# Attention keys in chunks of 512, six key products ahead, and another order on TensorE

## The chip, the cores and the metric

One core of one Trainium2 chip runs the whole program in one launch. The metric is the device time of an execution in microseconds (us), lower is better. Engines are called TensorE (PE in the profile, PEld its weight loads), VectorE (DVE), ScalarE (ACT), GpSimd (POOL) and SyncE (SP).

## What is computed

The reference is one block of three parts over x (2 sequences of 64 rows of 256) and a context (2 sequences of 1024 rows of 256). The change touches the first part alone, a cross attention with 16 heads of 64 and one learned null key and value:

```python
q = x_normed @ Wq;  k, v = split(ctx @ Wkv)
q, k = tanh(q), tanh(concat(null_key, k))
attn = softmax(q @ k.T * 64 ** -0.5)
x = x + (attn @ concat(null_value, v)) @ Wout + bout
```

Then follow a gated linear attention and a mixture of 8 experts (2 per row), each with its own normalisation and residual. Their code stays as it is.

## The kernel before

The attention never forms the values. For each head it sums the context rows themselves, weighted with the exponentials of the scores (mixT), and multiplies by the value weights once at the end (`values`, L1166).

The work is cut into **steps**. A unit is a batch b, a chunk c of CK = 256 keys and a group g of 8 heads; there are 16 units. Each unit has KT = 2 steps, one for each 128 keys, so there are 32 steps. Each step has three jobs on TensorE:

- `project_keys(kp)` (L1104), a **key product**: two head pairs by the chunk's 256 keys into one PSUM bank (two banks, in turn). Operands are split into a high and a low part, and three products (high-high, high-low, low-high; `split_product`, L1097) over two halves of the 256 inputs make 12 matmuls of 256 columns.
- `scores(s)` (L1123): 16 small f16 matmuls, 128 keys by the 8 heads' queries, into one of two score banks.
- `weighted_sum(s)` (L1140): 6 matmuls of 512 columns, split likewise, the context rows (ctx_h, ctx_l) by the exponentials (ex_h, ex_l), accumulated in four banks.

ScalarE follows with `keys_tanh` (L611: a tanh in PSUM and two copies to f16, the keys' high half) and `exponentials` (L654: the same exponential written twice). VectorE follows with `low_keys` (L793: the keys' low half, two instructions), `low_exponentials` (L849: the low part of the exponentials at L765, and their sum at L822), the casts of arriving context chunks to their high part (`high_ctx`, L778, for the weighted sums; `high_ctxT`, L771, transposed, for the key products) and `evacuate` (L804: finished sums out of PSUM). GpSimd makes the chunks' low parts (`low_ctx`, L518; `low_ctxT`, L514), in the order in which VectorE casts them. Chunks lie in two buffers each, in turn. SyncE issues their loads, between those of later weights.

Every engine's order is written out by hand; each runs its list in program order, and semaphores tie them. A key product waits until its bank's last keys have their low half (`k_ready`), a score step for its bank (`el_ready`, `esum_ready`), a weighted sum for the exponentials' low part and for its context chunk:

```python
                pe.wait_ge(el_ready, s + 1)
                pe.wait_ge(ctx_ready, n + 1)
```

Before the first score, AHEAD = 3 key products are done. The first four steps run singly: scores, a key product, a weighted sum (L1221). From then on TensorE's order in a pair of steps is scores, key products (three ahead), weighted sums of the pair before (L1231 to L1241). The pairs are numbered here from 0; pair u holds steps 2u and 2u+1, and is unit u. VectorE's list has the casts in `convert_context` (L857), behind each unit's low halves.

At the start x is normalised (VectorE, L762), transposed by TensorE, copied out of PSUM (`xnT`, L833) and multiplied by the query weights (L1200). TensorE fills the time before that with matmuls of no use (`warm`, L1086).

## Time and profile before

| | us |
|---|---|
| median of 3 runs | 204.99 |
| lowest and highest | 203.99, 205.06 |
| the profiled execution | 204.92 |
| its span in the profile | 203.0 |
| attention, first query product to the values | 8.0 to 124.2 |

The profile holds one execution. Its page gives busy times by engine and by line; its timelines give the start and duration of each instruction, with the idle time ahead of it and what ended that in brackets. Durations of matmuls overlap, since they are pipelined, so the distance between two starts tells what one costs in a stream.

### The profile page before, as it was taken

The numbers are of one execution on the slowest core, as the hardware profiler recorded it, in microseconds if no ns is written. First come the engines' busy times: TensorE is split into PE (matmuls) and PEld (weight loads), VectorE is DVE, ScalarE is ACT, GpSimd is POOL, SyncE is SP. The second block draws the span as 40 slices with busy tenths as digits, with TensorE's granted clock in tenths as the row PEclk, the third lists the DMA queues.
The fourth block names the chain that finished last, engine by engine and source line by source line (L and its number), as shares of the span: only waits on it lengthen the run. The fifth ranks groups of instructions, "written<-read, shape, count | busy, mean of one in ns | idle before, by whom it ended". The sixth has DMA issues, their size and how long they took to land.

```text
span 203.0 us, 4247 instructions
## 1 busy us (share of the span) xinstructions
PE 192.7 (95%) x1667; PEld 147.0 (72%) x1669; DVE 142.5 (70%) x259; ACT 116.2 (57%) x217; POOL 47.4 (23%) x48
## 2 busy tenths in 40 slices
PE   7999889999999999999999999999986999999991
PEld 2698779988998889988998767866753454544680
DVE  2679899989888899999878699435777825404313
ACT  2389999777977798778877672026430133222200
POOL 5636024220222062202202950021321300000001
PEclk9999999999999999999999999999999699999998
DMA  6945984934691110010000799999999400000000
GB/s 207 390 110 128 281 187 118 365 108 124 185 343 35 52 52 3 0 55 0 5 0 2 242 386 264 386 375 377 381 377 378 150 0 3 0 0 0 5 0 26
DMA packets 20836, 30.95 MB, mean 152 GB/s; under 512 B 1841, under 2 KB 15570, under 8 KB 20818
## 3 DMA queue, kind: packets, MB, share of 16 engines
q1 hardware_dynamic: 20098, 29.12, 44.1%
q10 hardware_dynamic: 720, 1.57, 2.1%
q8 instruction: 13, 0.21, 0.4%
q14 instruction: 5, 0.04, 0.1%
HBM read 29.51 MB, written 0.13 MB: 146 GB/s over the span
## 4 chain that ended last, share of the span: by engine, by line
PE 59%; issue 21%; DVE 11%; ACT 4%; POOL 2%; DMA 2%; POOLq 0%; DVEq 0%; ACTq 0%
PE ps L1101 39%; PE ps L1135 6%; PE ps L1200 2%; DVE keys L799 2%; PE ps L1175 2%; PE ps L1191 2%; PE ps L1089 2%; DVE att L949 2%; DMA x<-in_x 2%; DVE ex_sum L822 1%; ACT keys L621 1%; DVE ex_l L765 1%; PE ps L1163 1%; DVE lo L974 1%; PE ps L1312 1%
## 5 line engine op out<-in xcount | busy, mean ns | idle before, releaser
L799 DVE SCALAR_TENSOR_TENSOR keys<-ps,keys 64x512 f16<-64x512 f32 x64 | 44.1, 688 | 2.9 <-ACT keys L621 0.9
L621 ACT ACTIVATE keys<-ps 64x512 f16<-64x512 f32 x64 | 37.9, 593 | 1.8
L1101 PE MATMUL ps<-ctxT_h,w_k_h 128*128 128x256 f32 x128 | 37.9, 296 | 0.0
L1101 PE MATMUL ps<-ctxT_h,w_k_l 128*128 128x256 f32 x128 | 36.2, 282 | 0.0
L1101 PE MATMUL ps<-ctxT_l,w_k_h 128*128 128x256 f32 x128 | 36.1, 282 | 0.0
L765 DVE TENSOR_TENSOR ex_l<-ps,ex_h 128x512 fp32r<-128x512 f32 x32 | 22.0, 688 | 9.7 <-ACT ps L661 9.6
L660 ACT ACTIVATE ex_h<-ps 128x512 fp32r<-128x512 f32 x32 | 19.1, 597 | 13.9 <-PE ps L1135 13.7
L1101 PE MATMUL ps<-ex_h,ctx_h 128*128 128x512 f32 x64 | 25.3, 396 | 0.0
L1101 PE MATMUL ps<-ex_l,ctx_h 128*128 128x512 f32 x64 | 25.1, 392 | 0.0
L1101 PE MATMUL ps<-ex_h,ctx_l 128*128 128x512 f32 x64 | 24.9, 389 | 0.0
L1101 PEld LDWEIGHTS ps<-ctxT_h,w_k_h 128*128 128x128 f32 x128 | 24.4, 191 | 0.2
L1101 PEld LDWEIGHTS ps<-ctxT_l,w_k_h 128*128 128x128 f32 x128 | 24.5, 191 | 0.1
L1101 PEld LDWEIGHTS ps<-ctxT_h,w_k_l 128*128 128x128 f32 x128 | 24.4, 191 | 0.0
L822 DVE TENSOR_TENSOR ex_sum<-ex_sum,ps 128x512 f32<-128x512 f32 x32 | 21.7, 678 | 0.0
L1135 PEld LDWEIGHTS ps<-q_two,keys 128*128 128x128 f16 x512 | 16.0, 98 | 6.4 <-DVE keys L799 4.9
L505 POOL TENSOR_TENSOR ctx_l<-stage_n,ctx_h 128x512 fp32r<-128x512 f32 x8 | 10.3, 1294 | 42.4 <-DVE ctx_h L783 42.4
L1135 PE MATMUL ps<-q_two,keys 128*128 128x64 f16 x512 | 18.2, 193 | 1.8 <-DVE keys L799 1.1
L617 ACT ACTIVATE ps<-ps 128x512 f32<-128x512 f32 x32 | 18.4, 576 | 1.5 <-PE ps L1101 1.2
L661 ACT ACTIVATE ps<-ps 128x512 f32<-128x512 f32 x32 | 19.1, 598 | 0.0
L505 POOL TENSOR_TENSOR ctxT_l<-stage_t,ctxT_h 128x512 fp32r<-128x512 f32 x7 | 9.2, 1312 | 29.7 <-DVE ctxT_h L776 29.7
L1089 PE MATMUL ps<-warmer 128*128 128x512 bf16 x41 | 14.6, 500 | 1.5 <-POOL warmer L499 1.3
L1101 PEld LDWEIGHTS ps<-ex_h,ctx_h 128*128 128x128 f32 x64 | 12.1, 189 | 3.7 <-issue 1.6
(189 smaller groups left out, 272.9 us busy)
## 6 DMA issues: line engine op xcount, KB each, us to landing
w<-in_fc1T SPq DMA_DIRECT2D x8, 1024.0 KB, 12.4
w<-in_fc SPq DMA_DIRECT2D x8, 1024.0 KB, 12.3
stage_n<-in_ctx SPq DMA_DIRECT2D x8, 256.0 KB, 2.9
stage_t<-in_ctxT SPq DMA_DIRECT2D x7, 256.0 KB, 4.4
q_two<-q_split SPq DMA_DIRECT2D x8, 128.0 KB, 2.3
w_v<-in_Wv SPq DMA_DIRECT2D x1, 1024.0 KB, 5.4
w_out<-in_Wout SPq DMA_DIRECT2D x1, 1024.0 KB, 8.1
const<-in_const SPq DMA_DIRECT2D x1, 968.0 KB, 6.6
```

The lines of the kernel that those rows point to most:

```text
L505: return nc.gpsimd.tensor_tensor(dst, full, high.bitcast(F32), ALU.subtract)
L617: nc.scalar.activation(full, full, ACT.Tanh).then_inc(k_tanh, 1)
L621: nc.scalar.activation(keys[rows, u % 2, PK * i:PK * (i + 1), r], full[rows].rearrange("p (j n) -> p j n", j=PK), ACT.Copy, scale=UNIT).th ...
L660: nc.scalar.activation(ex_h[:, r], full, ACT.Exp, scale=SCORE_SCALE)
L661: nc.scalar.activation(full, full, ACT.Exp, scale=SCORE_SCALE).then_inc(e_ready, 1)
L765: return V.tensor_tensor(dst, full, high.bitcast(F32), ALU.subtract)
L799: V.scalar_tensor_tensor(out=keys[other, u % 2, PK * i:PK * (i + 1), r], in0=ps[mine, K_BANK + kp % 2].rearrange("p (j n) -> p j n", j=PK) ...
L822: V.tensor_tensor(total, total, ps[:, S_BANK + s % 2].rearrange("p (h q) -> p h q", q=S), ALU.add).then_inc(esum_ready, 1)
L949: V.copy_predicated(dst, mask, src).then_inc(att_ready, 1)
L1089: MM(ps[:, bank], warmer[:, 0:P], warmer[:], start=True, stop=True)
L1101: last = MM(dst, lhs[i], rhs[j], start=start and m == 0, stop=stop and m == len(parts) - 1)
L1135: last = MM(ps[:, S_BANK + s % 2, (2 * j + r) * S:(2 * j + r + 1) * S], keys[:, u % 2, j, r, t * P:(t + 1) * P], q_two[:, g, r, part, j, b ...
```

## The change

Key products and the transposed context now go by chunks of CK = 512 keys, so that there are 8 units of KT = 4 steps and still 32 steps. A key product is one head pair by 512 keys: 6 matmuls of 512 columns. The context rows of the weighted sums keep chunks of CN = 256 keys, eight of them, numbered over both batches; a weighted sum of step s reads chunk n = 2 (b NC + c) + t // 2. The key weights stay in four pieces, each now used by two key products.

AHEAD is 6, and all 16 pairs v run alike: TensorE does scores of steps 2v and 2v+1, weighted sums of steps 2v-2 and 2v-1, then key products 2v+6 and 2v+7. VectorE's casts and evacuations follow from three small tables, by the pair behind which they stand. The identity matrix is now loaded first from ScalarE's queue, no longer from SyncE's, and the copy of xnT is ScalarE's. The buffers for transposed chunks double in size.

```diff
@@ -40,14 +40,18 @@
...
-CK = 256
+CK = 512
+CN = 256
...
+NN = NK // CN
+KN = CN // P
...
+PIECES = 4
@@ -143,16 +147,16 @@
...
-        w_k_stage = alloc(attn_a, "w_k_stage", [P, G * KT, DC, PK * P])
+        w_k_stage = alloc(attn_a, "w_k_stage", [P, PIECES, DC, INNER // PIECES])
...
-        stage_n = alloc(attn_a, "stage_n", [P, 2, KT, D])
+        stage_n = alloc(attn_a, "stage_n", [P, 2, KN, D])
...
@@ -367,8 +371,8 @@
...
-        AHEAD = KT + 1
-        SINGLES = G * KT
+        AHEAD = KT + 2
+        PAIRS = STEPS // 2
@@ -400,7 +404,7 @@
...
         def ctx_source(n):
-            return a["ctx"][n * CK:(n + 1) * CK].rearrange("(t p) d -> p t d", p=P)
+            return a["ctx"][n * CN:(n + 1) * CN].rearrange("(t p) d -> p t d", p=P)
@@ -432,7 +436,6 @@
...
             sp.dma_start(x0[:], a["x"]).then_inc(ld_x, 16)
-            sp.dma_start(const[:, 0:C_ONES], a["eye"]).then_inc(ld_eye, 16)
@@ -451,12 +454,9 @@
...
-            load_ctxT(4)
             load_ctx(3)
...
-            load_ctxT(5)
-            load_ctx(4)
@@ -470,15 +470,13 @@
...
-            for n in range(5, B * NC):
-                if n + 1 < B * NC:
-                    load_ctxT(n + 1)
+            for n in range(4, B * NN):
                 load_ctx(n)
...
-                    sp.wait_ge(ctx_ready, B * NC)
+                    sp.wait_ge(ctx_ready, B * NN)
@@ -529,29 +527,31 @@
...
-                    for i in range(G * KT):
+                    for i in range(PIECES):
...
+                    low_ctx(0)
...
-                    low_ctx(0)
-                    for i in range(1, B * NC):
-                        if i + 1 < B * NC:
-                            low_ctxT(i + 1)
+                    low_ctx(1)
+                    pool.wait_ge(zero_ready, 1)
+                    pool.wait_ge(null_ready, 2)
+                    pool.wait_ge(ctx_ready, 2)
+                    for r in range(2):
+                        sums, mine = null_rows(1, r)
+                        nc.gpsimd.tensor_copy(sums, mine).then_inc(null_sums, 1)
+                    pool.wait_ge(null_sums, 2)
+                    low_ctxT(2)
+                    low_ctx(2)
+                    low_ctx(3)
+                    low_ctxT(3)
+                    low_ctx(4)
+                    pool.wait_ge(esum_ready, STEPS // B)
+                    pool.wait_ge(ctx_ready, 5)
+                    for r in range(2):
+                        sums, mine = null_rows(0, r)
+                        nc.gpsimd.tensor_tensor(sums, sums, mine, ALU.add).then_inc(null_sums, 1)
+                    pool.wait_ge(null_sums, 4)
+                    for i in range(5, B * NN):
...
-                        if i == 1:
-                            pool.wait_ge(zero_ready, 1)
-                            pool.wait_ge(null_ready, 2)
-                            pool.wait_ge(ctx_ready, i + 1)
-                            for r in range(2):
-                                sums, mine = null_rows(1, r)
-                                nc.gpsimd.tensor_copy(sums, mine).then_inc(null_sums, 1)
-                            pool.wait_ge(null_sums, 2)
-                        if i == NC:
-                            pool.wait_ge(esum_ready, STEPS // B)
-                            pool.wait_ge(ctx_ready, i + 1)
-                            for r in range(2):
-                                sums, mine = null_rows(0, r)
-                                nc.gpsimd.tensor_tensor(sums, sums, mine, ALU.add).then_inc(null_sums, 1)
-                            pool.wait_ge(null_sums, 4)
@@ -635,6 +635,7 @@
...
+            act.dma_start(const[:, 0:C_ONES], a["eye"]).then_inc(ld_eye, 16)
             act.dma_start(stage_t[:, 0], ctxT_source(0)).then_inc(ld_ctxT[0], 16)
@@ -642,6 +643,8 @@
...
             split_wk(0)
+            act.wait_ge(xnT_psum, 1)
+            copy(xnT[:], ps[:, 0, 0:DC * P].rearrange("p (c t) -> p c t", c=DC), xnT_ready)
             split_wk(1)
@@ -649,7 +652,8 @@
...
-            keys_tanh(2)
+            for kp in range(2, AHEAD):
+                keys_tanh(kp)
@@ -660,15 +664,12 @@
...
-            for s in range(SINGLES):
-                exponentials(s)
-                if s < G:
-                    null_exp(s)
-                keys_tanh(s + AHEAD)
-            for u in range(SINGLES // KT, NU):
-                for s in range(KT * u, KT * (u + 1)):
-                    exponentials(s)
-                for kp in range(KT * u + AHEAD, min(KT * (u + 1) + AHEAD, STEPS)):
+            for v in range(PAIRS):
+                exponentials(2 * v)
+                if v < G:
+                    null_exp(v)
+                exponentials(2 * v + 1)
+                for kp in range(2 * v + AHEAD, min(2 * v + AHEAD + 2, STEPS)):
                     keys_tanh(kp)
@@ -779,7 +780,7 @@
...
-                    dve.wait_ge(mix_done, G * KT * (n - 1))
+                    dve.wait_ge(mix_done, KT * (2 * ((n - 2) // 2) + 1) + KN * (n % 2) + KN)
@@ -829,8 +830,6 @@
...
-            dve.wait_ge(xnT_psum, 1)
-            V.tensor_copy(xnT[:], ps[:, 0, 0:DC * P].rearrange("p (c t) -> p c t", c=DC)).then_inc(xnT_ready, 1)
@@ -842,9 +841,11 @@
...
-            high_ctxT(1)
             high_ctx(0)
             low_keys(2)
+            high_ctxT(1)
+            for kp in range(3, AHEAD):
+                low_keys(kp)
@@ -854,27 +855,20 @@
...
-            def convert_context(u):
-                b, c, g = units[u]
-                n = b * NC + c
-                if g == 0 and n + 2 < B * NC:
-                    high_ctxT(n + 2)
-                if g == G - 1 and n + 1 < B * NC:
-                    high_ctx(n + 1)
-
-            for s in range(SINGLES):
-                low_exponentials(s)
-                low_keys(s + AHEAD)
-                if s % KT == KT - 1:
-                    convert_context(s // KT)
-            for u in range(SINGLES // KT, NU):
-                for s in range(KT * u, KT * (u + 1)):
+            next_ctx = {0: 1, 4: 2, 5: 3, 8: 4, 9: 5, 12: 6, 13: 7}
+            next_ctxT = {3: 2, 7: 3}
+            left = {7: 2, 9: 3}
+            for v in range(PAIRS):
+                for s in range(2 * v, 2 * v + 2):
                     low_exponentials(s)
-                for kp in range(KT * u + AHEAD, min(KT * (u + 1) + AHEAD, STEPS)):
+                for kp in range(2 * v + AHEAD, min(2 * v + AHEAD + 2, STEPS)):
                     low_keys(kp)
-                convert_context(u)
-                if units[u - 2][1] == NC - 1:
-                    evacuate(u - 2)
+                if v in next_ctxT:
+                    high_ctxT(next_ctxT[v])
+                if v in next_ctx:
+                    high_ctx(next_ctx[v])
+                if v in left:
+                    evacuate(left[v])
@@ -1109,14 +1103,15 @@
...
-                pe.wait_ge(wk_ready[KT * g + i], 1)
+                piece, half = 2 * g + i // 2, i % 2
+                pe.wait_ge(wk_ready[piece], 1)
...
-                    cols = slice(j * P, (j + 1) * P)
+                    cols = slice(half * P, (half + 1) * P)
...
-                                             [w[:, KT * g + i, d, cols] for w in (w_k_h, w_k_l)],
+                                             [w[:, piece, d, cols] for w in (w_k_h, w_k_l)],
@@ -1140,7 +1135,7 @@
...
-                n = b * NC + c
+                n = 2 * (b * NC + c) + t // KN
@@ -1148,7 +1143,7 @@
...
-                    last = split_product(ps[:, mix_bank(half, g)], [x[:, n % 2, t, cols] for x in (ctx_h, ctx_l)],
+                    last = split_product(ps[:, mix_bank(half, g)], [x[:, n % 2, t % KN, cols] for x in (ctx_h, ctx_l)],
@@ -1217,28 +1212,23 @@
...
-            project_keys(2)
-            for s in range(SINGLES):
-                scores(s)
-                if s < G:
-                    null_scores(s)
-                project_keys(s + AHEAD)
-                if s == KT:
-                    pe.wait_ge(null_ready, 1)
-                if s >= KT:
-                    weighted_sum(s - KT)
-            pe.wait_ge(null_ready, 2)
-            for u in range(SINGLES // KT, NU):
-                for s in range(KT * u, KT * (u + 1)):
-                    scores(s)
-                for kp in range(KT * u + AHEAD, min(KT * (u + 1) + AHEAD, STEPS)):
-                    project_keys(kp)
-                if u == NU - 1:
+            for kp in range(2, AHEAD):
+                project_keys(kp)
+            for v in range(PAIRS):
+                scores(2 * v)
+                if v < G:
+                    null_scores(v)
+                scores(2 * v + 1)
+                if v == PAIRS - 1:
...
                     denominators(0)
-                for s in range(KT * (u - 1), KT * u):
-                    weighted_sum(s)
+                if v >= 1:
+                    pe.wait_ge(null_ready, min(v, G))
+                    for s in range(2 * v - 2, 2 * v):
+                        weighted_sum(s)
+                for kp in range(2 * v + AHEAD, min(2 * v + AHEAD + 2, STEPS)):
+                    project_keys(kp)
@@ -1480,7 +1470,7 @@
...
-    arrays["Wk"] = v["L0_xattn_Wkv"][:, :INNER].reshape(DC, P, G * KT, PK * P).transpose(2, 1, 0, 3)
+    arrays["Wk"] = v["L0_xattn_Wkv"][:, :INNER].reshape(DC, P, PIECES, INNER // PIECES).transpose(2, 1, 0, 3)
```

TensorE's list from the end of pair 4 into pair 5, one row an instruction. L1101 (before) and L1095 (after) are the split products: with `ctxT` they are key products, with `ex` weighted sums; L1135 and L1130 are scores. Before:

```order
L1101 MATMUL ps<-ex_h,ctx_l 128x512
L1135 MATMUL ps<-q_two,keys 128x64 [waits esum_ready,el_ready,k_ready]
L1135 MATMUL ps<-q_two,keys 128x64 x15
L1135 MATMUL ps<-q_two,keys 128x64 [waits esum_ready,el_ready,k_ready]
L1135 MATMUL ps<-q_two,keys 128x64 x15
L1101 MATMUL ps<-ctxT_h,w_k_h 128x256 [waits k_ready,wk_ready1,ctxT_ready]
L1101 MATMUL ps<-ctxT_l,w_k_h 128x256
L1101 MATMUL ps<-ctxT_h,w_k_l 128x256
```

and with the change:

```order
L1095 MATMUL ps<-ctxT_h,w_k_l 128x512
L1130 MATMUL ps<-q_two,keys 128x64 [waits esum_ready,el_ready,k_ready]
L1130 MATMUL ps<-q_two,keys 128x64 x15
L1130 MATMUL ps<-q_two,keys 128x64 [waits esum_ready,el_ready,k_ready]
L1130 MATMUL ps<-q_two,keys 128x64 x15
L1095 MATMUL ps<-ex_h,ctx_h 128x512 [waits ctx_ready,el_ready,null_ready]
L1095 MATMUL ps<-ex_l,ctx_h 128x512
L1095 MATMUL ps<-ex_h,ctx_l 128x512
```

Behind the two score steps stood the key products; now the weighted sum stands there, with its wait for the context chunk (`ctx_ready`).

VectorE's list around the cast of context chunk 2 (it waits for the load `ld_ctx2`). Before:

```order
L765 TENSOR_TENSOR ex_l<-ps,ex_h 128x512 [waits mix_done,e_ready]
L822 TENSOR_TENSOR ex_sum<-ex_sum,ps 128x8x64 [waits esum_ready]
L799 SCALAR_TENSOR_TENSOR keys<-ps,keys 64x2x256 [waits k_high] x4
L783 CAST ctx_h<-stage_n 128x512 [waits mix_done,ld_ctx2]
L765 TENSOR_TENSOR ex_l<-ps,ex_h 128x512 [waits mix_done,e_ready]
L822 TENSOR_TENSOR ex_sum<-ex_sum,ps 128x8x64 [waits esum_ready]
L765 TENSOR_TENSOR ex_l<-ps,ex_h 128x512 [waits mix_done,e_ready]
L822 TENSOR_TENSOR ex_sum<-ex_sum,ps 128x8x64 [waits esum_ready]
L799 SCALAR_TENSOR_TENSOR keys<-ps,keys 64x2x256 [waits k_high] x4
L776 CAST ctxT_h<-stage_t 128x512 [waits k_psum,ld_ctxT4]
L765 TENSOR_TENSOR ex_l<-ps,ex_h 128x512 [waits mix_done,e_ready]
```

and with the change:

```order
L766 TENSOR_TENSOR ex_l<-ps,ex_h 128x512 [waits mix_done,e_ready]
L823 TENSOR_TENSOR ex_sum<-ex_sum,ps 128x8x64 [waits esum_ready]
L766 TENSOR_TENSOR ex_l<-ps,ex_h 128x512 [waits mix_done,e_ready]
L823 TENSOR_TENSOR ex_sum<-ex_sum,ps 128x8x64 [waits esum_ready]
L800 SCALAR_TENSOR_TENSOR keys<-ps,keys 64x512 [waits k_high] x4
L784 CAST ctx_h<-stage_n 128x512 [waits mix_done,ld_ctx2]
L766 TENSOR_TENSOR ex_l<-ps,ex_h 128x512 [waits mix_done,e_ready]
L823 TENSOR_TENSOR ex_sum<-ex_sum,ps 128x8x64 [waits esum_ready]
L766 TENSOR_TENSOR ex_l<-ps,ex_h 128x512 [waits mix_done,e_ready]
```

The cast stands behind four low halves in both, those of the two latest key products. With the change the next one (`ld_ctx3`) stands one pair later in place of two, and no cast of `ctxT` lies between.

## Rows read from the trace of the kernel before

**Rows 1.** the page: busy time by engine, clock in 40 slices

```profile
PE 192.7 (95%) x1667; PEld 147.0 (72%) x1669; DVE 142.5 (70%) x259; ACT 116.2 (57%) x217; POOL 47.4 (23%) x48
...
PEclk9999999999999999999999999999999699999998
```

**Rows 2.** busy time by stage, 60 to 70 us

```profile
60.00:70.00 10.00, 10.00 (x97) 8.65 (x96) 8.89 (x15) 8.08 (x15) 1.29 (x1) 1.00 0.24 77
```

**Rows 3.** timeline of TensorE; columns: start us, duration us

```profile
60.22 0.40 PE L1101 MATMUL ps<-ex_h,ctx_h 128*128 128x512 f32 x1
...
62.97 1.11 PE L1135 MATMUL ps<-q_two,keys 128*128 128x64 f16 x32
...
63.91 0.36 PE L1101 MATMUL ps<-ctxT_h,w_k_h 128*128 128x256 f32 x1
...
64.11 0.28 PE L1101 MATMUL ps<-ctxT_l,w_k_h 128*128 128x256 f32 x1
64.23 0.28 PE L1101 MATMUL ps<-ctxT_h,w_k_l 128*128 128x256 f32 x1
...
66.86 0.40 PE L1101 MATMUL ps<-ex_h,ctx_h 128*128 128x512 f32 x1
...
69.61 1.11 PE L1135 MATMUL ps<-q_two,keys 128*128 128x64 f16 x32
```

**Rows 4.** timeline of ScalarE in the steady stretch

```profile
37.06 0.60 ACT L660 ACTIVATE ex_h<-ps 128x512 fp32r<-128x512 f32 x1 [0.98 <-PE ps L1135]
...
38.07 0.59 ACT L660 ACTIVATE ex_h<-ps 128x512 fp32r<-128x512 f32 x1
...
39.07 0.56 ACT L617 ACTIVATE ps<-ps 128x512 f32<-128x512 f32 x1
...
40.90 0.58 ACT L617 ACTIVATE ps<-ps 128x512 f32<-128x512 f32 x1
```

**Rows 5.** timeline of VectorE from 38 us, and its evacuation at 77 us

```profile
38.18 0.69 DVE L765 TENSOR_TENSOR ex_l<-ps,ex_h 128x512 fp32r<-128x512 f32 x1 [0.37 <-ACT ps L661]
...
39.38 0.68 DVE L765 TENSOR_TENSOR ex_l<-ps,ex_h 128x512 fp32r<-128x512 f32 x1
...
40.69 2.85 DVE L799 SCALAR_TENSOR_TENSOR keys<-ps,keys 64x512 f16<-64x512 f32 x4
...
43.57 0.43 DVE L783 CAST ctx_h<-stage_n 128x512 fp32r<-128x512 f32 x1
...
77.27 1.29 DVE L809 COPY mixT<-ps 128x512 f32<-128x512 f32 x2
```

**Rows 6.** timeline of GpSimd, the low part of a context chunk

```profile
44.08 1.29 POOL L505 TENSOR_TENSOR ctx_l<-stage_n,ctx_h 128x512 fp32r<-128x512 f32 x1 [4.83 <-DVE ctx_h L783]
```

**Rows 7.** timeline of the start: VectorE, then TensorE

```profile
5.53 0.41 DVE L762 TENSOR_SCALAR xn<-x,stat 128x256 f32<-128x256 f32 x1 [0.45 <-POOL stat L530]
...
9.81 0.36 PE L1101 MATMUL ps<-ctxT_h,w_k_h 128*128 128x256 f32 x1
...
22.24 0.64 PE L1135 MATMUL ps<-q_two,keys 128*128 128x64 f16 x16 [0.73 <-DVE keys L799]
...
30.21 0.63 PE L1135 MATMUL ps<-q_two,keys 128*128 128x64 f16 x16 [0.58 <-DVE ex_sum L822]
```

**Rows 8.** DMA issues to 40 us: KB each, us from issue to landing

```profile
stage_t<-in_ctxT ACTq DMA_DIRECT2D x1, 256.0 KB, 3.4
```

**Rows 9.** busy time by stage, around the fall of the clock

```profile
154.00:157.00 3.00, 1.35 (x9) 0.73 (x8) 1.89 (x7) 0.39 (x1) 0.56 (x1) 1.00 1.01 387
157.00:161.00 4.00, 4.00 (x16) 1.90 (x16) 3.06 (x17) 0.30 (x2) 0.19 (x1) 0.57 0.68 219
```

**Rows 10.** timeline of TensorE, end of the attention

```profile
115.27 1.11 PE L1135 MATMUL ps<-q_two,keys 128*128 128x64 f16 x32 [0.41 <-DVE keys L799]
...
124.22 0.98 PE L1175 MATMUL ps<-mixT,w_v 128*64 128x128 f32 x14
```

More of the change, by code:

```diff
@@ L145, in block_kernel @@
         attn_a = ExitStack()
-        w_k_stage = alloc(attn_a, "w_k_stage", [P, G * KT, DC, PK * P])
+        w_k_stage = alloc(attn_a, "w_k_stage", [P, PIECES, DC, INNER // PIECES])
         stage_t = alloc(attn_a, "stage_t", [P, 2, DC, CK])
-        stage_n = alloc(attn_a, "stage_n", [P, 2, KT, D])
-        w_k_h = alloc(attn_a, "w_k_h", [P, G * KT, DC, PK * P], F32R)
-        w_k_l = alloc(attn_a, "w_k_l", [P, G * KT, DC, PK * P], F32R)
+        stage_n = alloc(attn_a, "stage_n", [P, 2, KN, D])
+        w_k_h = alloc(attn_a, "w_k_h", [P, PIECES, DC, INNER // PIECES], F32R)
+        w_k_l = alloc(attn_a, "w_k_l", [P, PIECES, DC, INNER // PIECES], F32R)
         ctxT_h = alloc(attn_a, "ctxT_h", [P, 2, DC, CK], F32R)
@@ L153, in block_kernel @@
         keys = alloc(attn_a, "keys", [P, 2, PG, 2, CK], F16)
-        ctx_h = alloc(attn_a, "ctx_h", [P, 2, KT, D], F32R)
-        ctx_l = alloc(attn_a, "ctx_l", [P, 2, KT, D], F32R)
+        ctx_h = alloc(attn_a, "ctx_h", [P, 2, KN, D], F32R)
+        ctx_l = alloc(attn_a, "ctx_l", [P, 2, KN, D], F32R)
         NE = 4
@@ L165, in block_kernel @@
         null_two = alloc(attn_a, "null_two", [P, 2, P], F16)
-        alloc(attn_a, "rest_of_seven_experts", [P, 5760])
+        alloc(attn_a, "rest_of_seven_experts", [P, 640])
         attn_b = ExitStack()
@@ L246, in block_kernel @@
         ld_wq = [sem(f"ld_wq{half}") for half in range(2)]
-        ld_wk = [sem(f"ld_wk{i}") for i in range(G * KT)]
-        ld_ctx = [sem(f"ld_ctx{n}") for n in range(B * NC)]
+        ld_wk = [sem(f"ld_wk{i}") for i in range(PIECES)]
+        ld_ctx = [sem(f"ld_ctx{n}") for n in range(B * NN)]
         ld_ctxT = [sem(f"ld_ctxT{n}") for n in range(B * NC)]
@@ L276, in block_kernel @@
         wk_later = sem("wk_later")
-        wk_ready = [sem(f"wk_ready{i}") for i in range(G * KT)]
+        wk_ready = [sem(f"wk_ready{i}") for i in range(PIECES)]
         ctxT_high = sem("ctxT_high")
```

## The prediction

> **What bounds the kernel now.** I read four views, in this order. First the page: TensorE is busy for 192.7 of 203.0 us, far ahead of VectorE (142.5) and ScalarE (116.2) [rows 1]. That share is an average over stages, so I next took the busy times of a stretch inside the attention. From 60 to 70 us TensorE is busy for all 10.00 us, VectorE for 8.89 and ScalarE for 8.08, at the full clock [rows 2]. So TensorE sets the pace, with only a tenth of the time to spare behind it.
>
> Third, TensorE's timeline shows where its time goes [rows 3]. A duration there overlaps the next instruction, so I take distances between starts. Twelve 512-column matmuls of two weighted sums run from 60.22 to 62.97: 2.75 us, 0.229 each. Two score steps take 0.94 (62.97 to 63.91). Two key products, 24 matmuls of 256 columns, take 2.95 (63.91 to 66.86), at 0.12 each (64.11 to 64.23) and some 0.08 once behind the scores. A pair of steps thus takes 6.64 (62.97 to 69.61), and it does so from pair 3 to pair 14 without a stall. Fourth, the other engines' timelines give the chain behind a key product. ScalarE needs 1.01 us for the two exponentials of a step (37.06 to 38.07) and 1.83 for the tanh and the two copies of a key product (39.07 to 40.90) [rows 4]. VectorE needs 1.20 for low part and sum of a step (38.18 to 39.38), 2.85 for the four low halves of two key products, 0.43 for a cast of 128x512, 1.29 for an evacuation [rows 5]. GpSimd needs 1.29 for the low part of such a chunk [rows 6].
>
> **Wide key products.** 384 matmuls of 256 columns become 192 of 512. At 0.12 and 0.229 that is 46.1 against 44.0 us: **2.1 us less**, on the engine that sets the end. The spacing of 0.229 is that of the weighted sums, same type and columns. The Trainium skill (TensorE: Matmul & The Clock Gate, section Back-to-back issue gap) gives columns over 2.4 GHz plus 2.5 ns, that is 109 and 216 ns. By it this term would be only 0.5 us (192 times 2.5 ns). The case's spacings are wider than the page's, and more so for the narrow form, so the sum stays with the rows.
>
> **The new order, and a wait that it brings.** This decides. In pair v TensorE now runs scores, then the weighted sums of pair v-1, and the key products last. VectorE casts a context chunk at the end of its pair v, behind the low halves of exactly those last key products. The table puts chunk 2 behind pair 4, and the weighted sum of step 8, the first to read it, is the first thing after the scores in pair 5. The same holds for chunk 3 (pair 5, read in pair 6), 4 (8, 9), 5 (9, 10) and 6 (12, 13). Chunk 1 is cast a pair earlier than needed, and chunk 7 follows a pair without key products; these two don't wait.
>
> Let 0 be the start of the scores of the next pair. The second key product is really finished at 0.16 (a 512-column matmul lasts 0.40 but is followed after 0.23 [rows 3]), the first 1.37 before it. ScalarE takes the first from -1.2 to 0.65, the second to 2.5 [rows 4]. VectorE's last low half ends at 3.2, the cast at 3.7 [rows 5], GpSimd's low part at 5.0 with 0.08 between them [rows 6]. TensorE has finished the scores at 0.95 [rows 3]. It waits **4.1 us**, and behind the waiting weighted sum stand the next key products, so nothing of it is made up: the chain starts anew from them. With a ScalarE that is free at once the chain would be 0.5 shorter (3.6). In pair 9 it is longer: behind pair 7 VectorE has a cast of 1024 columns (0.86) and an evacuation (1.29), 2.1 us together, of which I reckon 0.9 reach TensorE through a late score bank and a late cast. Four times 4.1 and once 5.0 are **21.4 us** more. In the kernel before, chunk 2's cast (43.57 [rows 5]) has its low part ready at 45.4 [rows 6], and its first reader comes after the key products of pair 5: that pair starts two times 6.64 ahead of 62.97 [rows 3], at 49.7, so the reader at 53.6. These 8 us of cover are gone.
>
> **The clock.** From 154 to 157 us TensorE is busy for 1.35 of 3.00 us, and from 157 to 161 its mean granted clock is 0.57: it has gone from 2.4 to 1.2 GHz for most of that stretch, and 0.43 of 4.0 us, 1.7 us of its work, are lost [rows 9]. Five waits of 4.1 us are longer than those gaps. Each may cost from 0 (the clock holds) to 1.7. I take 1.3, since part of the slow stretch will lie in the wait itself: **6.5 us** more.
>
> **The start.** The first load has twice the keys. The old one landed 3.4 us after its issue [rows 8]; I estimate 1.3 us more, since 0.25 MB more stand ahead. VectorE converts it before it normalises x (5.53 [rows 7]), which moves that by about 1 us. The copy of the transposed x goes to ScalarE, which takes part of this back, as does the loading of the query weights one place earlier. The first key product (9.81 [rows 7]) should start at about 10.3. Then six key products stand before the first score, TensorE at 1.38 each, ScalarE at 1.83. TensorE waits for banks before the fifth (1.4), the sixth (0.9) and the fourth score step (0.5): 2.8, in place of some 1.9 before, of which two are shown [rows 7]. With 0.5 and 0.9, less what the better filled pipe gives back, I take **1.2 us** more, between 0 and 3.
>
> **The end.** Before, TensorE waits 0.41 us ahead of the last scores [rows 10]; with the wait in pair 13 VectorE is ahead there: **0.4 less**. The last key products end two pairs earlier, but from the last scores to the values (115.27 to 124.22 [rows 10]) the program is the same, as it is behind them.
>
> **At nothing:** the casts and low parts of doubled width (same elements in all, GpSimd is busy for 47.4 us of 203 [rows 1]), the fewer DMA issues on SyncE, the removed single steps, GpSimd's new order. The doubled cast of the transposed context is covered by a pair of key products; without that cover it costs about 2 us twice. The expert loads wait for the same last chunk and keep their distance to the end.
>
> **Sum:** -2.1 + 21.4 + 6.5 + 1.2 - 0.4 = 26.6 on the profiled execution's 204.92 (span 203.0 and 1.9 around it), 231.5. The median of the runs is 204.99, 0.07 above, within their spread.
>
> **The rivals.** *The clock holds.* The same five waits, without 6.5: 225.0. For it: the waits are short against the 6.6 us of dense work between them. Against: rows 9, where less idle time was enough. *No waits for chunks.* VectorE would have to reach the casts 4.1 us earlier. Then pair 8 to 10 and the pairs without key products would be VectorE-bound instead: I reckon 1.0 and 1.7 us of late score banks, and the time is 204.9 - 2.1 + 1.2 - 0.4 + 2.7 = 206.3. Against it stands the written order. *Faster.* TensorE streams without any wait: the chunk's casts are early enough, and six key products ahead remove the waits of before, 1.9 at the start and 0.4 at the end. Price: -2.1 - 2.3, so 200.5. It decides from the point where cast and low part are done within the 0.95 us of scores; for it speaks that ScalarE has 1.9 us in ten free, against it the chain above, whose shortest form is still 3.6 us too long. *Part of the waits*, because one or two of the five chunks come in time: about 215.
>
> **How the numbers follow.** The forecast has 0.65, the held clock 0.17, part of the waits 0.07, no waits 0.06, faster 0.05. About 0.5% (1 us) is what a measurement can tell from no change. No waits is 0.7% slower, near that line, so I give 0.03 of it to the same. Faster 0.05, same 0.03, slower 0.92. The range: low end with the held clock, the short chain (five times 3.6) and no loss at the start, 220.5; high end with 1.7 for each clock fall and 3 at the start, 235.3. From 220 to 236 holds the first two cases, 0.82.
>
> **What would show it.** Right: five idle stretches of some 4 us on TensorE ahead of the weighted sums' first matmul, released by GpSimd's low part of a context chunk, in pairs 5, 6, 9, 10 and 13; a pair without a wait of 6.5 us; five low stretches in the clock row. Wrong: no such idle time, or the clock at full throughout, or a first key product later than 11 us.

## The result

| us | before | after |
|---|---|---|
| median (4 runs each) | 204.98 | 237.57 |
| lowest and highest | 203.99, 205.06 | 236.94, 238.88 |
| the profiled execution | 204.92 | 236.94 |
| its span | 203.0 | 234.9 |
| its mean granted clock | 0.989 | 0.935 |
| first query product | 8.00 | 8.10 |
| start of the values | 124.22 | 157.09 |

The ratio on record is 1.163, between 1.159 and 1.167; the quotient of the two medians in the table is 1.159. Runs more than 1.5% above the fastest of the same version, which came up in three of the versions below, are left out of the comparisons. The forecast was 231.5, in a range of 220 to 236: the direction and the mechanism came true, and the time lies 1.6 us above the range.

The page after, which answers to [rows 1]: busy time by engine, the granted clock in 40 slices of 5.9 us, and the costliest group of TensorE.

```profile
PE 202.0 (86%) x1475; PEld 144.3 (61%) x1477; DVE 141.6 (60%) x254; ACT 117.5 (50%) x218; POOL 45.1 (19%) x44
...
PEclk9999999999595899859589988999999999999999
...
L1095 PE MATMUL ps<-ex_h,ctx_h 128*128 128x512 f32 x64 | 31.2, 488 | 20.9 <-POOL ctx_l L503 20.9
```

TensorE's share fell from 95 to 86%, and the clock row, full in the attention before, has five dips. Five stretches of idle time account for it. The third line says where they lie: ahead of the weighted sums' first matmuls, 20.9 us, all put down to GpSimd's low part of the context rows. The view of waits gives the count: five, the longest 4.2.

```profile
PE ps L1095 <- POOL ctx_l L503: 20.9, 5, 4.2
PE ps L1095 <- DVE keys L800: 2.1, 3, 1.4
PE ps L1130 <- DVE ex_sum L823: 0.8, 2, 0.6
```

TensorE's timeline in pairs 5 and 6, answering to [rows 3] (start, duration; L1130 are scores, `ex` weighted sums, `ctxT` key products; in brackets the idle time ahead and what ended it):

```profile
54.48 1.11 PE L1130 MATMUL ps<-q_two,keys 128*128 128x64 f16 x32
59.76 0.77 PE L1095 MATMUL ps<-ex_h,ctx_h 128*128 128x512 f32 x1 [4.17 <-POOL ctx_l L503]
60.32 0.63 PE L1095 MATMUL ps<-ex_l,ctx_h 128*128 128x512 f32 x1
60.75 0.63 PE L1095 MATMUL ps<-ex_h,ctx_l 128*128 128x512 f32 x1
...
64.16 0.54 PE L1095 MATMUL ps<-ex_l,ctx_h 128*128 128x512 f32 x1
64.54 0.39 PE L1095 MATMUL ps<-ex_h,ctx_l 128*128 128x512 f32 x1
64.77 0.40 PE L1095 MATMUL ps<-ctxT_h,w_k_h 128*128 128x512 f32 x1
...
67.54 0.64 PE L1130 MATMUL ps<-q_two,keys 128*128 128x64 f16 x16
...
72.80 0.77 PE L1095 MATMUL ps<-ex_h,ctx_h 128*128 128x512 f32 x1 [4.16 <-POOL ctx_l L503]
```

Two losses stand here, one behind the other. The reader of chunk 2 starts 5.28 us after its pair, in place of 0.95. And then its matmuls start 0.43 us apart (60.32 to 60.75), in place of 0.23, until 64.54. The busy times by stage give the clock (length of the stretch, then busy time of TensorE with its count of matmuls, of its weight loads, VectorE, ScalarE and GpSimd, then the mean granted clock):

```profile
54.00:57.60 3.60, 1.59 (x35) 1.18 (x33) 3.08 (x5) 3.47 (x7) 0.58 (x1) 1.00 0.00 0
57.60:64.40 6.80, 4.64 (x11) 3.74 (x12) 3.12 (x6) 1.49 (x4) 1.27 (x1) 0.50 0.15 39
64.40:68.00 3.60, 3.60 (x30) 2.82 (x30) 0.40 (x1) 1.58 (x3) 0.00 (x0) 0.99 0.00 0
...
112.40:119.00 6.60, 5.54 (x13) 4.41 (x14) 3.21 (x6) 0.33 (x1) 0.91 (x1) 0.50 0.17 42
139.60:142.80 3.20, 2.84 (x7) 2.31 (x8) 1.72 (x4) 0.00 (x0) 1.62 (x3) 0.50 0.00 0
```

In pair 5 the mean granted clock is 1.00, then 0.50 (1.2 GHz) for 6.8 us, of which TensorE works 4.64, then 0.99 again. At half speed 4.6 us of work lose 2.3. The other four falls differ. In pairs 6, 9 and 10 the low stretch is as long but lies later against the wait, so that 5.2 to 5.5 us of it are work (the fourth line is pair 10). In pair 13 it lasts 3.3 us, with 2.8 of work (the last line).

The chain behind the wait, from the timelines of VectorE and GpSimd, which answer to [rows 5, 6]:

```profile
56.40 1.41 DVE L800 SCALAR_TENSOR_TENSOR keys<-ps,keys 64x512 f16<-64x512 f32 x2 [0.42 <-ACT keys L621]
57.84 0.43 DVE L784 CAST ctx_h<-stage_n 128x512 fp32r<-128x512 f32 x1
...
58.35 1.27 POOL L503 TENSOR_TENSOR ctx_l<-stage_n,ctx_h 128x512 fp32r<-128x512 f32 x1 [3.77 <-DVE ctx_h L784]
```

Pair 5 starts at 54.48. The last low half ends at 3.3 us behind it, the cast at 3.8, the low part at 5.1, the reader starts at 5.3.

The starts of the pairs give the sum. A pair without a wait takes 6.51, before 6.64. Pairs 5, 6, 9, 10 and 13 take 13.06, 13.32, 14.04, 13.54 and 9.51 (the last has no key products, 3.8 without a wait). That is 33.6 more than without. Their readers start 5.28, 5.26, 5.99, 5.34 and 5.27 behind the pair's start; less 0.95 each, the waits are **22.4 us**. The other **11.2** are the low clock: 2.2, 2.5, 2.5, 2.6 and 1.4 in the five pairs. Behind the values the program took 1.0 us less than before: the fall of the clock of [rows 9] did not come in this execution. The kernel before has executions of both kinds too. Of 17 that were run beside the later versions, the eight with a granted clock of 0.994 or more took 203.8 to 204.1 us, the nine with 0.988 or 0.989 took 204.2 to 205.2, and the profiled one (204.92) is of the second kind. So this 1.0 us is probably scatter and not the change's doing.

### The profile page after: what moved, and what is told of

It is laid out like the page before. It is cut to its first block, busy times and chain, and to the rows that moved or that the text cites. A ratio compares the mean times of both kernels' runs of the same rounds, so it can differ in the third digit from the quotient of the medians.

```text
span 234.9 us, 3848 instructions
## 1 busy us (share of the span) xinstructions
PE 202.0 (86%) x1475; PEld 144.3 (61%) x1477; DVE 141.6 (60%) x254; ACT 117.5 (50%) x218; POOL 45.1 (19%) x44
## 4 chain that ended last, share of the span: by engine, by line
PE 49%; issue 21%; DVE 14%; ACT 8%; POOL 4%; DMA 2%; ACTq 0%; POOLq 0%; DVEq 0%
PE ps L1095 35%; DVE keys L800 5%; PE ps L1130 4%; ACT keys L621 3%; ACT ps L617 3%; POOL ctx_l L503 3%; DMA w_k_stage<-in_Wk 2%; PE ps L1170 2%; PE ps L1186 1%; DVE att L943 1%; PE ps L1083 1%; DVE ctx_h L784 1%; PE ps L1195 1%; PE ps L1158 1%; DVE lo L968 1%
## 5 line engine op out<-in xcount | busy, mean ns | idle before, releaser
L1095 PE MATMUL ps<-ex_h,ctx_h 128*128 128x512 f32 x64 | 31.2, 488 | 20.9 <-POOL ctx_l L503 20.9
L1095 PEld LDWEIGHTS ps<-ex_h,ctx_h 128*128 128x128 f32 x64 | 14.5, 227 | 25.7 <-issue 23.0
L1095 PE MATMUL ps<-ex_l,ctx_h 128*128 128x512 f32 x64 | 29.1, 455 | 0.0
L1095 PE MATMUL ps<-ex_h,ctx_l 128*128 128x512 f32 x64 | 29.1, 455 | 0.0
L1095 PE MATMUL ps<-ctxT_h,w_k_h 128*128 128x512 f32 x64 | 25.7, 402 | 2.1 <-DVE keys L800 2.1
L1095 PE MATMUL ps<-ctxT_h,w_k_l 128*128 128x512 f32 x64 | 25.0, 391 | 0.0
L1095 PE MATMUL ps<-ctxT_l,w_k_h 128*128 128x512 f32 x64 | 25.0, 390 | 0.0
L1130 PEld LDWEIGHTS ps<-q_two,keys 128*128 128x128 f16 x512 | 16.2, 98 | 6.1 <-issue 5.6
L1130 PE MATMUL ps<-q_two,keys 128*128 128x64 f16 x512 | 18.3, 193 | 0.8 <-DVE ex_sum L823 0.8
L1095 PEld LDWEIGHTS ps<-ex_h,ctx_l 128*128 128x128 f32 x64 | 14.6, 228 | 3.7
L1095 PEld LDWEIGHTS ps<-ex_l,ctx_h 128*128 128x128 f32 x64 | 14.8, 232 | 2.8
L1095 PEld LDWEIGHTS ps<-ctxT_h,w_k_h 128*128 128x128 f32 x64 | 12.4, 194 | 5.9 <-issue 3.4
L1384 PE MATMUL ps<-w,xd 128*64 128x512 f32 x64 | 14.6, 598 | 0.0
```

The source lines that it names most:

```text
L1095: last = MM(dst, lhs[i], rhs[j], start=start and m == 0, stop=stop and m == len(parts) - 1)
L1130: last = MM(ps[:, S_BANK + s % 2, (2 * j + r) * S:(2 * j + r + 1) * S], keys[:, u % 2, j, r, t * P:(t + 1) * P], q_two[:, g, r, part, j, b ...
L1384: last = MM(ps[SLOTS * j:SLOTS * (j + 1), half], xd[:, c, e * SLOTS:(e + 1) * SLOTS], w1[e][:, c, half * 512:(half + 1) * 512], start=c == ...
```

## The experiments

The theory after the result: late casts make the waits (22.4 us), and each wait brings a fall of the clock (11.2 us in all). The first rival was that the new order makes VectorE or ScalarE the bound, wherever the casts stand; the second that the casts are too late in any order; the third that the slow matmuls come from something else than the waits, such as contention of VectorE and GpSimd on the chunk's buffers.

### Casts one pair earlier

```diff
-            next_ctx = {0: 1, 4: 2, 5: 3, 8: 4, 9: 5, 12: 6, 13: 7}
+            next_ctx = {0: 1, 3: 2, 4: 3, 7: 4, 8: 5, 11: 6, 12: 7}
```

> The changed kernel with chunks 2 to 6 (and 7) of the context cast one pair earlier on VectorE, nothing else. Theory (the five waits are the place of the casts in VectorE's list): all five waits and all low stretches of the clock go; the five pairs took 33.7 us more than 6.51 (or 3.77) us, so 237.6 - 33.7 = 203.9, plus up to 2.7 us of late score banks: 203.9 to 206.6. Rival (VectorE or ScalarE would be the bound of the new order, the cast is only where it shows): at least half of it stays, over 220.

Measured: 207.49, the median of three runs (a fourth, of 211.05, is left out), ratio 1.017 (1.012 to 1.022). One table line gives back 30 of the 32.6 us. It is 0.9 above the theory's upper end of 206.6, and far below the rival's 220. TensorE's waits in it:

```profile
PE ps L1130 <- DVE ex_sum L823: 3.0, 5, 1.3
...
PE ps L1095 <- DVE keys L800: 2.1, 3, 1.4
...
PE ps L1095 <- POOL ctx_l L503: 0.4, 1, 0.4
```

The 20.9 us for chunks are 0.4, and most pairs take 6.51. VectorE's load now shows as late score banks, 3.0 in place of 0.8, as the rival "no waits for chunks" had it (2.7).

### Key products second

The casts stay late; TensorE's order in a pair becomes scores, key products, weighted sums, as in the kernel before.

```diff
+                for kp in range(2 * v + AHEAD, min(2 * v + AHEAD + 2, STEPS)):
+                    project_keys(kp)
                 if v >= 1:
                     pe.wait_ge(null_ready, min(v, G))
                     for s in range(2 * v - 2, 2 * v):
                         weighted_sum(s)
-                for kp in range(2 * v + AHEAD, min(2 * v + AHEAD + 2, STEPS)):
-                    project_keys(kp)
```

> The changed kernel with TensorE's order scores, key products, weighted sums; casts where they stand. Theory: the key products stand in front of the reader of the chunk again; the low part is ready some 1.5 us ahead of it, so no waits: 204 to 207. Rival (the casts are too late in any order): 215 and more.

Measured: 206.9, ratio 1.012 (1.007 to 1.017), no wait for a chunk. Two edits at different ends of the same dependence each remove the loss, so it is the combination of order and table that costs.

### The waits filled

Ahead of the weighted sums of pairs 5, 6, 9, 10 and 13 stand 19 bf16 matmuls of 512 columns with weights of zero, added to a bank of sums, so that TensorE works while it would wait. (In pair 9, whose bank begins new sums, the first of them waits for the old ones to be copied out and clears it. GpSimd zeroes their weights at the start and builds the matrix that lies there behind the attention.)

```diff
+                if v in (5, 6, 9, 10, 13):
...
+                    for _ in range(19):
+                        MM(ps[:, mix_bank(0, 0)], strict_b[:], warmer[:], ...)
```

> The changed kernel with 19 matmuls of 512 columns whose weights are zero (they add nothing) in front of the first weighted sum of pairs 5, 6, 9, 10 and 13, so that TensorE works through the waits. The waits on GpSimd's low part stay, the clock should hold. Theory (waits 22.4, clock 11.3 us): 237.6 - 11.3 = 226.3, clock 0.99. Rival (the clock is not what makes the matmuls behind the wait slow, or its term is the 6.5 us of the prediction): 231 or more.

Measured: 227.17, ratio 1.113 (1.108 to 1.119), 10.4 us less than the changed kernel, and 0.9 above the theory's 226.3. TensorE in pair 5:

```profile
54.50 1.11 PE L1132 MATMUL ps<-q_two,keys 128*128 128x64 f16 x32
55.66 4.05 PE L1233 MATMUL ps<-warmer,strict_b 128*128 128x512 bf16 x18
59.78 0.47 PE L1097 MATMUL ps<-ex_h,ctx_h 128*128 128x512 f32 x1
60.09 0.40 PE L1097 MATMUL ps<-ex_l,ctx_h 128*128 128x512 f32 x1
60.32 0.39 PE L1097 MATMUL ps<-ex_h,ctx_l 128*128 128x512 f32 x1
...
65.33 0.84 PE L1132 MATMUL ps<-q_two,keys 128*128 128x64 f16 x23
```

The weighted sum starts at the same place (5.28 behind the pair's start), but the matmuls behind it are 0.23 apart, and the pair takes 10.83 in place of 13.06. VectorE and GpSimd do the same work at the same time in both, so contention falls as the cause. The five pairs take 10.83, 10.84, 11.54, 10.88 and 8.12, that is 22.4 us more than without waits, and the values start at 145.86, 11.2 us earlier than in the changed kernel. This splits the loss of the attention: 22.4 us of waiting, 11.2 of clock. The total falls by less, 10.4, since behind the values this execution has a fall of the clock that the changed kernel's had not, worth 1.0 us there (78.84 us from the values to the end, against 77.81):

```profile
179.00:182.00 3.00, 3.00 (x10) 1.30 (x10) 2.07 (x14) 0.30 (x2) 0.00 (x0) 0.50 0.76 241
```

### The cast between the two low halves

```diff
                     low_keys(kp)
+                    if v in next_ctx and v > 0 and kp % 2 == 0:
+                        high_ctx(next_ctx[v])
...
-                if v in next_ctx:
+                if v in (0, 13):
```

> The changed kernel with the casts of chunks 2 to 6 between the low halves of the pair's two key products, so 1.85 us earlier. The five waits shrink to some 2.4 us. If the clock falls as before: 237.6 - 5 x 1.85 = 228.3, or somewhat more if the low stretch lies more in the work. If it holds with waits of 2.4 us: 217.

Measured: 221.51, 16 us below the changed kernel, in a single run that can be compared (a second, of 225.19, is left out). The starts of pairs 5 to 7 (54.48, 63.45, 74.05):

```profile
54.48 1.11 PE L1132 MATMUL ps<-q_two,keys 128*128 128x64 f16 x32
57.91 0.47 PE L1097 MATMUL ps<-ex_h,ctx_h 128*128 128x512 f32 x1 [2.33 <-POOL ctx_l L503]
63.45 1.11 PE L1132 MATMUL ps<-q_two,keys 128*128 128x64 f16 x32
66.88 0.47 PE L1097 MATMUL ps<-ex_h,ctx_h 128*128 128x512 f32 x1 [2.32 <-POOL ctx_l L503]
...
74.05 1.11 PE L1132 MATMUL ps<-q_two,keys 128*128 128x64 f16 x32
```

The wait is cut from 4.2 to 2.3, as the chain says. Pair 5 takes 8.97, that is 6.51 and the wait: the clock held. Pair 6 with the same wait takes 10.60, with the clock at 0.50 from 67.7 to 71.1 us, behind the wait's end. The clock row of this run (40 slices of 5.5 us) dips for pairs 6, 9 and 13 (from 63, 87 and 121 us), and stays full for 5 and 10:

```profile
PEclk9999999999996999889999979999999999999998
```

So neither case of the expectation holds: a wait of 2.3 us (2.7 in pair 9) sometimes brings the clock down. Where it fell it stayed low for 3.4 us and cost 1.2 to 1.6.

### One chunk early

```diff
-            next_ctx = {0: 1, 4: 2, 5: 3, 8: 4, 9: 5, 12: 6, 13: 7}
+            next_ctx = {0: 1, 3: 2, 5: 3, 8: 4, 9: 5, 12: 6, 13: 7}
```

> The changed kernel with the cast of chunk 2 alone one pair earlier. Theory (each wait stands by itself: a wait and a low stretch of the clock, and the chain starts anew behind it): pair 5 falls from 13.06 to about 6.6 us and pair 6 stays at 13.3, so 237.6 - 6.5 = 231.1. Rival (the first wait lets the later ones come about, or the time lost moves to the next pair): over 234 or under 225.

Measured: 231.19, ratio 1.130 (1.125 to 1.136). As expected (231.1), and the waits add up singly; one is worth 6.4 us. In the parts the expectation was off: pair 5 takes 7.09 in place of 13.06, and not 6.6, and pair 6 did not stay at 13.3. It still waits 4.17 (67.27), but takes 12.43: the same wait lost 1.6 of clock in place of 2.5.

### Narrow key products

The casts early, and each key product again 12 matmuls of 256 columns in place of 6 of 512.

```diff
-                for j in range(PK):
+                for j in range(2):
+                    own = slice(j * 256, (j + 1) * 256)
...
-                        last = split_product(ps[:, K_BANK + kp % 2, j * CK:(j + 1) * CK],
+                        last = split_product(ps[:, K_BANK + kp % 2, own],
...
-                                             [x[:, n % 2, d, :] for x in (ctxT_h, ctxT_l)], d == 0, d == DC - 1)
+                                             [x[:, n % 2, d, own] for x in (ctxT_h, ctxT_l)], d == 0, d == DC - 1)
```

> The version with all casts a pair earlier, its key products as 12 matmuls of 256 columns in place of 6 of 512, all else equal. Theory (rows of the kernel before: 0.12 against 0.229): pair period 6.51 + 0.13 = 6.64 and 2 us more than that version: ratio to the kernel before 1.017 + 0.010 = 1.027. By the spacing that the notes give for isolated matmuls it would be 0.5 us, 1.019.

Measured: 208.68, ratio 1.021 (1.017 to 1.025), which is 1.2 us above the wide form. The period of a pair is 6.65 in place of 6.51, 0.14 for two key products, as the spacings of [rows 3] gave (2.1 us over 16 pairs); but the values start only 1.15 us later, probably since slower products shorten TensorE's waits for VectorE. The Trainium skill's spacing for an isolated matmul (TensorE: Matmul & The Clock Gate, section Back-to-back issue gap) would make it 0.03 a pair, an estimate; here the trace decides against it. The overlap of the two ratios' intervals leaves the total unproven; the period shows the price.

### Five key products ahead

The key products second, and `AHEAD = KT + 1`.

> The changed kernel with TensorE's order scores, key products, weighted sums and five key products ahead in place of six. Against the same order with six (ratio 1.012): the first score comes one key product earlier at the start, and the key products end one pair later, which takes away part of the 1.5 us wait for the exponentials' low part in the last pairs. Theory: 1 to 2 us less, ratio 1.003 to 1.008. Rival (ScalarE's rate sets the start whatever the order, and nothing is gained): 1.012.

Measured: 206.64, ratio 1.012 (1.007 to 1.017), a miss: no less than with six. Its profiled execution reached the values 1.6 us sooner, but 0.9 of that is an earlier start of the queries (7.95 and 8.82), which differs from one execution to the next.

### The first loads, five kernels

First the kernel before with nothing but this change's two edits at the start: the identity on ScalarE's queue, the copy of `xnT` on ScalarE.

```diff
-            sp.dma_start(const[:, 0:C_ONES], a["eye"]).then_inc(ld_eye, 16)
...
+            act.dma_start(const[:, 0:C_ONES], a["eye"]).then_inc(ld_eye, 16)
...
+            act.wait_ge(xnT_psum, 1)
+            copy(xnT[:], ps[:, 0, 0:DC * P].rearrange("p (c t) -> p c t", c=DC), xnT_ready)
...
-            dve.wait_ge(xnT_psum, 1)
-            V.tensor_copy(xnT[:], ps[:, 0, 0:DC * P].rearrange("p (c t) -> p c t", c=DC)).then_inc(xnT_ready, 1)
```

> The kernel before with the other first loads alone: the identity from ScalarE's queue, and the copy of the transposed x on ScalarE. Theory: x lands some 0.5 us earlier and its normalised form too; the first key product starts up to 0.5 us earlier, of which ScalarE's rate at the start takes part back: ratio 0.997 to 1.0. Rival: the copy delays ScalarE's own list and it is slower, 1.003.

Measured: a median of 206.59 over four runs, ratio on record 1.012 (1.006 to 1.018). But two of the four (207.33 and 207.93) are of those left out of comparisons. The other two, 204.23 and 205.86, have a mean of 205.0, against 204.5 for the kernel before, whose own runs lie 1.2 us apart. So a cost of the two edits is not shown, and neither of the expectations is decided. The profiled execution has the queries at 8.29 and the values at 124.53, 0.3 later than before. The scatter was reason enough to take the edits apart. The identity alone:

> The kernel before with only the identity matrix moved to ScalarE's queue, xnT still copied by VectorE. The identity now stands ahead of the first context chunk in that queue. If the identity is what moves the first instructions: queries at 8.2 to 8.4 us in place of 8.00, and a ratio of 1.001 to 1.003, below what 5 rounds can tell. If the scatter of the two edits together came from the start, this shows part of the 1.2%.

Measured: 204.59, ratio 1.000 (0.998 to 1.003). It costs nothing. Then both edits undone in the two versions with key products second, which have the large first chunk:

> The version with key products second (0.9 to 1.2% slower than before) with the identity matrix again loaded by SyncE and xnT again copied by VectorE. If the start's reordering by itself costs the 1.2% that the kernel before lost with it alone, this comes back to 0.998 to 1.003 of before. Rival: the change of loads costs little and its 1.2% was the clock's scatter behind the attention; then this stays at 1.008 to 1.013, from the 1.5 us wait of the last score steps for VectorE.

> The same with five key products ahead. The candidate to beat the kernel before: key products 2.1 us cheaper by the rows, the wait at the end of the attention 0.9 us. If the loads were what ate it: 0.992 to 0.999. If not: 1.005 to 1.012.

Measured: 209.45, ratio 1.026 (1.023 to 1.029), against 1.012 with the changed loads; and 207.91, ratio 1.019 (1.016 to 1.021), also against 1.012. Both expectations have the wrong sign: with a first chunk of 512 keys, the changed order of the loads is a gain of 1.3 and 0.7%. The start with six ahead, old loads (VectorE, TensorE, then busy time by stage):

```profile
4.96 0.43 DVE L755 BATCH_NORM_STATS2 stat<-x 128x6 f32<-128x256 f32 x1 [4.96 <-DMA x<-in_x]
...
6.84 1.35 DVE L761 TENSOR_SCALAR xn<-x,stat 128x256 f32<-128x256 f32 x1 [0.45 <-POOL stat L529]
...
8.33 0.41 PE L1088 MATMUL ps<-const,xn 128*128 128x128 f32 x2 [1.81 <-DVE xn L761]
...
13.12 0.48 PE L1095 MATMUL ps<-ctxT_h,w_k_h 128*128 128x512 f32 x1
...
10.00:13.00 3.00, 3.00 (x15) 3.00 (x15) 0.82 (x2) 0.00 (x0) 0.44 (x1) 0.50 0.63 230
```

and with the changed loads:

```profile
3.31 0.43 DVE L757 BATCH_NORM_STATS2 stat<-x 128x6 f32<-128x256 f32 x1 [3.31 <-DMA x<-in_x]
...
6.44 0.41 DVE L763 TENSOR_SCALAR xn<-x,stat 128x256 f32<-128x256 f32 x1
...
6.99 0.41 PE L1088 MATMUL ps<-const,xn 128*128 128x128 f32 x2 [0.38 <-DVE xn L763]
...
10.63 0.48 PE L1095 MATMUL ps<-ctxT_h,w_k_h 128*128 128x512 f32 x1
...
10.00:13.00 3.00, 3.00 (x18) 2.59 (x18) 2.88 (x5) 1.26 (x3) 1.08 (x1) 1.00 0.71 272
```

With the large chunk issued at 0.74, at the same time as x, x lands at 4.96; with the identity ahead of the chunk, at 3.31. The normalised x is ready 1.34 us later. Only 0.40 of that is a later start of VectorE's instruction (6.84 against 6.44); the rest is its duration of 1.35 in place of 0.41, beside a GpSimd instruction on the key weights that starts at 6.77. Why it takes longer there is not shown. TensorE waits 1.81 us for it, and its clock is 0.50 from 10 to 13 us, just when the query products run. The first key product behind them starts 2.5 us later: 0.9 because the query products start later (9.71 and 8.82), 1.6 because they take 3.4 us in place of 1.8. With five ahead and the old loads the profiled execution, the longest of its seven (210.41), has the clock at 0.50 even from 9.5 to 15.5 us. The kernel before, whose first chunk has half the size, has x at 3.92, and at 3.15 with the identity moved: there it is early enough either way.

At last the version that the runs pointed to: five ahead, changed loads, the copy of `xnT` on VectorE ahead of the chunk's low part, and chunk 6 cast behind pair 11.

```diff
-            act.wait_ge(xnT_psum, 1)
-            copy(xnT[:], ...)
+            dve.wait_ge(xnT_psum, 1)
+            V.tensor_copy(xnT[:], ...)
             dve.wait_ge(first_high, 1)
...
-            next_ctx = {0: 1, 4: 2, 5: 3, 8: 4, 9: 5, 12: 6, 13: 7}
+            next_ctx = {0: 1, 4: 2, 5: 3, 8: 4, 9: 5, 11: 6, 13: 7}
```

> Key products second, five ahead, the changed loads, with two more edits: xnT copied by VectorE ahead of the low part of the first transposed chunk (on ScalarE the copy waits behind the high part of the first weights, up to 1.0 us of TensorE's time at 7.8 to 8.8), and context chunk 6 cast behind pair 11 instead of 12 (0.8 us of waiting in pair 13). Theory: the ratios of 1.012 came from the copy's late and varying start and from the late waits; then the values start at 124 to 124.7 us and the ratio is 0.999 to 1.005. Rival: what is lost lies in the first loads themselves, which land late with the larger chunk whatever is done behind them; then 1.007 to 1.012. Neither theory expects it to beat the kernel before by more than can be measured.

Measured: 206.6, ratio 1.011 (1.009 to 1.014): the rival. Moving the copy to VectorE and chunk 6 one pair earlier makes no difference that can be measured (206.64 without them). And the wait of 0.8 us stayed, since it is chunk 7's, cast behind pair 13, and not chunk 6's; I had misread which chunk its reader uses.

## Why the prediction was wrong, and where it was right

By the parts of the sum, against the profiled execution's start of the values (124.22 to 157.09, 32.9 later):

| term | forecast | measured |
|---|---|---|
| wide key products | -2.1 | -2.1 (0.13 to 0.14 a pair) |
| five waits for chunks | 21.4 | 22.4 |
| the clock | 6.5 | 11.2; by filling the waits 11.2 too |
| the start (what is left over) | 1.2 | 1.4 |
| the end | -0.4 | -0.3 |
| a late score bank in pair 8 | - | 0.2 |
| behind the values | 0 | -1.0 |

- **The clock is the step that failed.** The forecast took 1.3 for each fall, and 1.7, the loss in [rows 9], as the most. That stretch was one event behind less idle time. Behind four of the five waits of 4.2 us the clock stayed at 1.2 GHz for 6.8 us, in the kernel before for 3.5 (157.4 to 161.0). I also reasoned that part of the slow stretch would lie in the wait: 1.2 to 2.2 us did, but 4.6 to 5.5 were left for work, and these pairs lost 2.2 to 2.6 each. Only pair 13, with a low stretch of 3.3 us, lost 1.4, about what I had taken. In all it is 11.2, 4.7 above the forecast and 2.7 above five times my bound, more than the 1.6 by which the time misses the range. The size of one event, behind a shorter stall, is no upper bound.
- **The wait** came in the five pairs named, released by the engine named. Four of them are 0.2 to 0.3 longer than 4.1: the last low half came at 3.3 in place of 3.2 and the reader 0.14 behind the low part. Pair 9 has 5.04, for 5.0. That VectorE's cast of 1024 columns and the evacuation would reach TensorE there was right; it shows as the reader's offset of 5.99 with 0.57 of it as a late score bank.
- **Wide products**: right by the period of a pair, undone in a run of its own.
- **The start**: the normalised x came 1.0 us later (6.52 against 5.53), as forecast, but the first key product at 9.91, only 0.1 later than before, forecast 10.3; pair 3 came at 41.46. Waits of 1.35 and 0.54 us ahead of the fifth and sixth product were forecast at 1.4 and 0.9. The forecast called the change of loads a thing that takes part back; in the version with key products second the old loads are 2.5 worse, with five ahead 1.3.
- **Behind the values** I had nothing. The profiled execution of the kernel before has a fall of the clock there that costs it about 1 us, and the changed one's has not; by the two kinds of execution named above this is probably scatter, and it hid 1 us of the miss.
- **The rivals.** *The clock holds* was refuted by the trace and its price of 225.0 confirmed by the filled waits (227.17; 1.2 of the 2.2 above it are the waits' and the start's excess in the table). *No waits for chunks*, 206.3, is what the early casts gave: 207.49, with the VectorE-bound pairs that were named. *Faster*: none of the versions was; see below.

Why does no version with wide products beat the kernel before, though they save 2.1 us? Scores of a unit need all its key products: with 512 keys four of 1.38 us stand before the first score, with 256 keys two. Four ahead wasn't run: with key products second, a unit's last product would end 2.75 us ahead of its scores, and its low halves are done only 3.2 us behind its end. Filling the five costs waits of 0.20, 1.33, 0.45 and 0.71 us in the last version, 2.7 in all, where the kernel before has 0.73 and 0.58 (and 0.36 ahead of the query products). Its pair 3 starts at 41.09, the kernel before's at 36.38; two more products explain 2.8 of these 4.7. The 0.13 a pair gained from there on, some 1.4 us, doesn't quite pay for the other 1.9, and the 0.8 for chunk 7 comes on top. The profiled execution reaches the values at 125.69, against 124.22, and takes 206.6 against 204.92, 0.8% more. The ratio is 1.1%, mostly because the profiled execution of the kernel before is one of its longer ones: the 11 runs beside this version have a median of 204.19.

**Open:** whether the copy of `xnT` on ScalarE costs the kernel before anything; two runs that can be compared are too few, and the copy alone wasn't run there. Also open is why VectorE's normalisation took 1.35 us with the old loads, and what decides whether the clock falls in a wait of 2.3 us.

## What to carry to other kernels

Before a consumer is moved forward in an in-order queue, look up behind what its producer's last step stands in the other queue: here a single row of a table, one pair earlier, was worth 30 us. Price a stall of TensorE twice, once for the wait and once for the slow clock behind it, and take the second from the longest comparable stall there is (here 1.4 to 2.6 us behind each wait of 4.2); if there is none, leave the top of the range open. A larger first tile delays everything issued with it and lengthens the filling of the pipeline, so weigh its saving per pass against both.

## What was not expected of the hardware

- During each idle stretch of 4.2 us TensorE's clock fell to 1.2 GHz, 2.0 to 3.8 us after it began. It stayed there for 6.8 us in four of the five, 4.6 to 5.5 of them full of work, and for 3.3 in the fifth. So the same wait cost between 1.4 and 2.6 us in one execution.
- Waits of 2.3 to 2.7 us brought it down in three cases of five in one execution, once only 0.8 us after the wait was over.
- 19 matmuls of 512 columns with zero weights, put into each wait, kept the clock at 1.00 there and gave back 11.2 us by the start of the values.
- x, first in its own queue, landed at 4.96 us with the 512 KB chunk first in the other one, at 3.92 with 256 KB, and at 3.31 or 3.15 once the identity stood ahead of the chunk.
- Idle stretches of 1.81 and then 0.54 us at the start were followed by a clock of 0.50 from 10 to 13 us, and 2.15 and 1.61 us by one from 9.5 to 15.5; waits of 1.09 to 1.58 us at the same place, in five other versions, were followed by none.
